# Router logits with stationary weights in four column groups, and a split first batch

## The reference

```
x = x + 0.5 * ffn(layernorm(x))          # router + 8 experts
x = x + attention(layernorm(x))          # 16 heads of 16, rms norm and rope on q and k
x = x + 0.5 * ffn(layernorm(x))          # the same router and experts again
ffn:  logits = x @ w_switch + b_switch   # (8192, 256) @ (256, 8)
      probs  = softmax(logits); routes = argmax; pos = rank of the token within its expert
      kept if pos < 512; y = relu(x @ w1[e] + b1[e]) @ w2[e] + b2[e], else y = x
attention: q, k, v = x @ wq.T, ...; q, k = rope(rms(q)), rope(rms(k))
      softmax(q k^T / 4 + 1) v, heads joined, @ wproj.T
```

## Time and profile before

| | us |
|---|---|
| median of 3 runs | 2403.99 (2400.88 to 2405.43) |
| the profiled execution | 2410.09 |
| its span, first to last instruction | 2408.2 |
| PE busy | 2194.1 (91%) |
| DVE busy | 1735.6 (72%) |
| ACT busy | 1731.4 (72%) |
| POOL busy | 977.8 (41%) |

### The profile page before, as it was taken

One profiled execution on the slowest core, in us unless ns is written; L12 is line 12 of the kernel. 1 busy time (PEld: TensorE's weight loads), 2 busy tenths in 40 slices (PEclk: granted clock), 3 DMA queues, 4 the chain that ended last, 5 costly groups with the idle time before them and its releaser, 6 DMA issues.

```text
span 2408.2 us, 36923 instructions
## 1 busy us (share of the span) xinstructions
PE 2194.1 (91%) x13224; PEld 1160.7 (48%) x13224; DVE 1735.6 (72%) x2555; ACT 1731.4 (72%) x3390; POOL 977.8 (41%) x1157
## 2 busy tenths in 40 slices
PE   6759974699899999999999999999999999996997
PEld 6738963343344434434444343444444334344896
DVE  5637755578788888798888779878887988413674
ACT  5846654358788788788878878887887887844663
POOL 3764423163273256239226623922751101113442
PEclk9999996599899999999999999999999999998998
DMA  5734331513344334334433434443343334101431
GB/s 201 261 100 172 137 105 49 91 28 82 80 81 109 57 82 101 73 58 108 98 59 86 90 76 60 98 96 59 76 106 58 68 59 107 49 17 63 158 106 62
DMA packets 144904, 218.33 MB, mean 91 GB/s; under 512 B 32225, under 2 KB 100955, under 8 KB 144465
## 3 DMA queue, kind: packets, MB, share of 16 engines
q1 hardware_dynamic: 135504, 199.01, 34.6%
q0 software_dynamic: 9216, 16.95, 2.0%
HBM read 129.59 MB, written 84.80 MB: 89 GB/s over the span
## 4 chain that ended last, share of the span: by engine, by line
PE 74%; DVE 10%; POOL 5%; issue 4%; ACT 4%; DMA 2%; SPq 1%; POOLq 0%; DVEq 0%; ACTq 0%
PE PS L800 18%; PE PS L784 17%; PE PS L767 10%; DVE NMX L1352 5%; PE PS L712 5%; PE PS L584 4%; PE PS L744 3%; PE PS L683 2%; PE PS L681 2%; PE PS L682 2%; POOL buf L1477 2%; PE PS L665 2%; PE PS L667 2%; PE PS L666 2%; PE PS L616 2%
## 5 line engine op out<-in xcount | busy, mean ns | idle before, releaser
L1352 DVE TENSOR_REDUCE NMX<-PS 128x1 f32<-128x1024 f32 x1024 | 1224.2, 1219 | 293.1 <-PE PS L767 287.7
L1043 ACT ACTIVATE PB<-PS 128x512 f32<-128x512 f32 x2048 | 1105.2, 605 | 229.6 <-PE PS L784 222.0
L784 PE MATMUL PS<-QF,KF 51*128 51x512 f32 x2048 | 802.9, 462 | 15.4 <-DMA QF<-MT 7.7
L767 PE MATMUL PS<-KF,QF 49*128 49x512 f32 x2048 | 727.5, 450 | 40.8 <-DVE NMX L1352 25.0
L784 PEld LDWEIGHTS PS<-QF,KF 51*128 51x128 f32 x2048 | 330.2, 185 | 558.2 <-ACT PB L1043 280.5
L800 PE MATMUL PS<-PB,V 128*17 128x512 f32 x4096 | 543.0, 602 | 0.2
L767 PEld LDWEIGHTS PS<-KF,QF 49*128 49x128 f32 x2048 | 317.6, 189 | 173.3 <-DVE NMX L1352 107.3
L1458 POOL TENSOR_TENSOR RS<-VE,NEGH 128x8 f32<-128x8 f32 x24 | 40.2, 1676 | 373.9 <-DVE VE L1148 373.9
L1279 DVE TENSOR_TENSOR HLR<-HL,HHR 128x512 fp32r<-128x512 f32 x128 | 88.6, 693 | 88.2 <-ACT HHR L973 88.2
L1569 POOL TENSOR_TENSOR R1R<-R,HI 128x512 fp32r<-128x512 f32 x56 | 71.7, 1282 | 183.1 <-ACT R L1010 183.1
L681 PE MATMUL PS<-W2H,HLR 128*128 128x256 f32 x512 | 143.1, 279 | 0.0
(11 more groups left out here) (173 smaller groups left out, 3331.2 us busy)
## 6 DMA issues: line engine op xcount, KB each, us to landing
W<-in_w SPq DMA_DIRECT2D x32, 1024.0 KB, 8.0
QF<-qs SPq DMA_DIRECT2D x192, 128.0 KB
KF<-qs SPq DMA_DIRECT2D x192, 128.0 KB
qs<-HI SPq DMA_DIRECT2D x64, 256.0 KB, 2.1
qs<-R1R SPq DMA_DIRECT2D x64, 256.0 KB, 2.5
buf<-ZT SPq DMA_DIRECT2D x16, 520.0 KB, 9.8
BUF<-buf SPq DMA_DIRECT2D x16, 520.0 KB, 8.5
PX<-x2d SPq DMA_DIRECT2D x8, 1024.0 KB, 5.4
```

The lines of the kernel that those rows point to most:

```text
L767: m = e.matmul(PS[:, 2 * i + half, :], QF[k][at:at + ROWS_S, p * SEQ + ti * 128:p * SEQ + ti * 128 + 128], KF[k][at:at + ROWS_S, p * SEQ + ...
L784: e.matmul(PS[:, bank, :], KF[k][at:at + ROWS_ST, p * SEQ + sbk * 128:p * SEQ + sbk * 128 + 128], QF[k][at:at + ROWS_ST, p * SEQ + th * 51 ...
L1043: e.activation(PB[j % 3][:, h * 512:(h + 1) * 512], PS[:, place["e", tile], :], ACT.Exp).then_inc(e_out, 1)
L1352: e.tensor_reduce(NMX[:, u % 2, at:at + 1], PS[:, 2 * i:2 * i + 2, :], AX.XY, ALU.max, negate=True).then_inc(s_max, 1)
```

## The change

Five things, in the diff below, cut to its core.

1. Logits: the router's weights, padded with zeros to 32 columns, are the stationary operand, once per group of 256 tokens in one of the four column groups of PE, and the transposed tokens move (256 columns). All four groups stand together at one step (`logits`); ACT copies the 128x256 result to LT, PE transposes it back in two blocks at the step `back`, and DVE's addition of the bias reads PSUM. What follows is one step later in `LATER`. The second routing's transposed tokens go to XTP instead of XTQ; the first's alternate between XTP and XTP2.
2. Batch 0's pieces: those that units 0 and 1 need (rows j = 0 and 2 of both halves) are at steps 40 to 43 of the preparation, the other four at steps 0, 1, 2, 4 of the main loop, with LO on POOL. Unit 0's load follows the first four pieces. Both halves are scaled after the second root.
3. Batch 1's preparation begins at step 4, batch 2's at step 55; `load_px` of batch 1 waits for six pieces. Values are 1 to 2 steps earlier, for batch 2 five.
4. QK has three buffers for two; `rope_out` and `sp_lo` have one semaphore per half.
5. `AGAIN_AT`: 42 matmuls after steps 13 to 21 become 26 after steps 17 to 20.

```diff
-SPLIT_AT = ((29, 31, 37, 39), (41, 43, 45, 47))
-VALUES_AT = (53, 55, 57, 59)
-FIRST_SPLIT = 4
+VALUES_AT = (52, 54, 56, 57)
+PIECES = ((29, 0, 0), (31, 0, 1), (37, 0, 2), (39, 0, 3), (41, 1, 0), (43, 1, 1), (45, 1, 2), (47, 1, 3))
+PIECES_0 = ((40, 0, 0), (41, 0, 2), (42, 1, 0), (43, 1, 2), (0, 1, 1), (1, 1, 3), (2, 0, 1), (4, 0, 3))
+BEGIN = {1: 4, 2: 55, **{b: BATCH * (b - 1) - EARLY for b in range(3, 8)}}
 FIRST = Way(...
-            logits=[9 + g for g in range(4)], shift=14, ...
+            logits=11, back=13, shift=14, ...
 LATER = Way(...
-            logits=[LEAVE + t for t in (5, 7, 9, 10)], shift=LEAVE + 11, ...
+            logits=LEAVE + 10, back=LEAVE + 11, shift=LEAVE + 12, ...
-AGAIN_AT = {**{n: 7 for n in range(13, 16)}, 16: 2, 17: 6, 18: 2, 19: 6, 20: 1, 21: 4}
+AGAIN_AT = {17: 7, 18: 7, 19: 7, 20: 5}
+def values_at(b, g):
+    return VALUES_AT[g] - (4 if b == 2 else 0) if b else BATCH - 5 + g
...
             def load_px(b):
                 if b:
-                    e.wait_ge(sp_full, 8 * b)
+                    e.wait_ge(sp_full, 8 * b if b > 1 else 6)
...
             def load_unit(u):
                 for i in range(2):
-                    e.wait_ge(st_q[i], 128 * (b + 1))
+                    e.wait_ge(st_q[i], 64 if u < 2 else 128 * (b + 1))
...
             def before(b):
-                for hf in range(2):
-                    for j in range(4):
-                        yield split_at(b, hf, j) + 3
-                        store_q(b, hf, j)
-                if b:
-                    yield EARLY + 52 if b > 1 else 56
+                yield from stores(b) if b else stores(b, 0, 4)
+                if b == 0:
+                    load_unit(0)
+                else:
+                    yield BATCH * (b - 1) + (52 if b > 1 else 57) - BEGIN[b]
                     load_unit(4 * b)
...
             def route(c):                                   # PE
-                for g in range(4):
-                    yield way.logits[g]
-                    e.wait_ge(xtq_out, 4 * c + g + 1)
-                    for i in range(2):
-                        for ch in range(2):
-                            m = e.matmul(PS[:, bank, i * 8:i * 8 + 8], xtq(c, g)[:, ch, i * 128:(i + 1) * 128],
-                                         WSW[:, ch, :], start=(ch == 0), stop=(ch == 1))
+                yield way.logits
+                e.wait_ge(xtq_out, 4 * c + 4)
+                for ch in range(2):
+                    for g in range(4):
+                        m = e.matmul(PS[32 * g:32 * g + 32, bank, 0:256], WSW[:, ch, :], xtq(c, g)[:, ch, :],
+                                     start=(ch == 0), stop=(ch == 1))
+                m.then_inc(lg_full, 1)
+                yield way.back
+                e.wait_ge(lg_out, c + 1)
+                transposes(bank, [LT[:, j * 128:(j + 1) * 128] for j in range(2)]).then_inc(lt_full, 1)
...
             def route(c):                                   # ACT
-                    e.copy(SM[k][:, 1, g * 16:g * 16 + 16], PS[:, lg_bank(c, g), 0:16]).then_inc(lg_out, 1)
+                e.copy(LT[:, :], PS[:, lg_bank(c), 0:256]).then_inc(lg_out, 1)
...
-                if n >= 2:
-                    e.wait_ge(rope_free, n - 1)
-                e.copy(QK[:, t % 2, :], PS[:, bank, :]).then_inc(qk_out, 1)
+                if n >= 3:
+                    e.wait_ge(rope_free, n - 2)
+                e.copy(QK[:, n % 3, :], PS[:, bank, :]).then_inc(qk_out, 1)
...
             def pre_x(b):                                   # DVE, batch 0
-                    if kk == 3 and b == 0:
-                        yield ROOT_AT[hf] + 1
+                if b == 0:
+                    yield ROOT_AT[1] + 1
+                    for hf in range(2):
                         e.wait_ge(rq_root, hf + 1)
                         for i in range(4):
-                            scale(e, n - 3 + i)
+                            scale(e, 4 * hf + i)
...
             for n in range(NS + LAST):                      # every engine
                 if n == 0:
-                    prepare(side, 0, 1, pre_x, values, split)
-                if r == BATCH - EARLY and b + 2 < NB:
-                    prepare(side, n, b + 2, pre_x, values, split)
+                    side.begin(n, split(0, 4, 4))
+                    prepare(side, BEGIN[1], 1, pre_x, split, values)
+                for k in range(2, NB):
+                    if n == BEGIN[k]:
+                        prepare(side, n, k, pre_x, split, values)
```

More of the change, by code:

```diff
@@ L116, in run, with pieces, prepare @@
         self.live = [s for s in self.live if s[1] is not None]
-def split_at(b, hf, j):
-    return SPLIT_AT[hf][j] + (FIRST_SPLIT if b == 1 else 0)
-def prepare(side, n, b, pre_x, *parts):
+def values_at(b, g):
+    return VALUES_AT[g] - (4 if b == 2 else 0) if b else BATCH - 5 + g
+def pieces(b, first=0, count=8):
+    table = PIECES if b else PIECES_0
+    for k in range(first, first + count):
+        at, hf, j = table[k]
+        yield k, at, hf, j, sum(p[1] == hf for p in table[:k])
+def prepare(side, n, b, pre_x, split, values=None):
     side.begin(n, pre_x(b))
-    for part in parts:
+    side.begin(n, split(b) if b else split(b, 0, 4))
+    if values is not None:
         for g in range(4):
-            side.begin(n, part(b, g))
+            side.begin(n, values(b, g))
 def build_program(nc, NB, x_in, wqkv, wproj, gq, wsw, bsw, w1, b1, w2, b2, cst, out):
@@ L714, in projected, with split @@
                 return m
-            def split(b, j):
-                for hf in range(2):
-                    yield split_at(b, hf, j)
-                    n = 8 * b + 4 * hf + j
-                    e.wait_ge(rope_out, 8 * b + 4 * hf + 4)
-                    bank = ring("split", n)
+            def split(b, first=0, count=8):
+                for k, at, hf, j, m in pieces(b, first, count):
+                    yield at
+                    e.wait_ge(rope_out[hf], 4 * b + 4)
+                    bank = ring("split", 8 * b + k)
                     take(bank)
                     transposes(bank, [QR[:, 4 * hf + i, j * 128:(j + 1) * 128] for i in range(4)]).then_inc(sp_full, 1)
-                    busy[bank] = (sp_raw, n + 1)
+                    busy[bank] = (sp_raw, 8 * b + k + 1)
             def values(b, g):
-                yield VALUES_AT[g]
+                yield values_at(b, g)
                 e.wait_ge(xt_lo, 4 * b + g + 1)
@@ L999, in pre_x, with split @@
                     e.activation(SQ[:, :], PS[:, bank, :], ACT.Square).then_inc(qk_sq, 1)
-            def split(b, j):
-                for hf in range(2):
-                    n = 8 * b + 4 * hf + j
-                    yield split_at(b, hf, j)
+            def split(b, first=0, count=8):
+                for k, at, hf, j, m in pieces(b, first, count):
+                    n = 8 * b + k
+                    yield at
                     e.wait_ge(sp_full, n + 1)
@@ L1397, in vector_program @@
                 if n == 0:
-                    prepare(side, 0, 1, pre_x, split)
-                if r == BATCH - EARLY and b + 2 < NB:
-                    prepare(side, n, b + 2, pre_x, split)
+                    side.begin(n, split(0, 4, 4))
+                    prepare(side, BEGIN[1], 1, pre_x, split)
+                for k in range(2, NB):
+                    if n == BEGIN[k]:
+                        prepare(side, n, k, pre_x, split)
                 if r == 0 and b >= 1:
```

156 lines of the change are left out of this document (83 added, 73 removed).

## The result

The changed kernel took 2365.81 us (median of 4 runs, 2361.95 to 2367.98) beside 2404.71 for the kernel before (2400.88 to 2409.74) on the same chip: ratio 0.9835, 95% interval [0.9812, 0.9858]. The forecast was 2359.4, with a range of 2343 to 2378. The profiled span went from 2408.2 to 2366.2 us.

What follows compares the result with a forecast made beforehand. Bounds were taken by stretch: TensorE full in later batches (203 of 207 us), waits exposed in batch 0's preparation. Terms -6.6 - 14 - 9 - 14 - 1 = -44.6 took 2404.0 to 2359.4 us, range 2343 to 2378.

Steps and rivals of the forecast that it cites:

- First routing: Before the first scatter: new logits blocks let ScalarE go on sooner, so the first scatter comes earlier, -6.6 us.
- Preparation: Batch 0's exposed preparation: eight tiles without a pause, four pieces left instead of six, unit 0's load earlier, -14 us.
- eight in a row: Batch 0's preparation: VectorE turns eight tiles without a stop, one per 2.59 us, from 375.4 to 396.1.
- standing alone: Unit 0's load in batch 0's preparation: 13.6 us, given no gain for running without other loads beside it.
- Rival B: Steps 0 to 8 of batch 0 give the preparation's gain back while TensorE's clock is low: 2370 us, chance 0.12.
- Batch 0: Batch 0's attention: stall near 600 us gone (-11), added transposes (+2), fewer matmuls (-1.7), later projections (+1.5): together -9 us.
- move with BEGIN, nothing changes: Batch 0's attention: batch 1's statistics shift with its preparation's start, priced at nothing.
- rival D: Stall near 600 us stays: maxima's load still late behind the store before it, only -3 of -11, 2367 us, chance 0.08.
- Later batches: Seven later batches: new logits spare TensorE 2.7 us each, partly hidden by VectorE's statistics; 2.0 taken per batch, -14 us.
- The tiling rule: Logits blocks: a change of tiling mode drains TensorE; already within the 0.98, or 0.8 us lost over seven batches.
- Tail: Last batch's exposed logits, after attention: last copy 1.5 earlier, without groups between, -1 us.
- Rival C: Batch 0 from step 17: fewer matmuls fail to raise the clock; thirty slow steps give 2437 us, chance 0.04.

Runs made afterwards that it cites:

- Run 1: Changed kernel with the old logits in both routings, the rest of the change kept: ratio 0.9889, batches 1 to 5 207.1 to 207.4 us.
- run 8: Changed kernel with POOL's first root of batch 0 waiting for the eighth sum instead of the fourth: 84.8 us from PX to the first maximum.
- run 3: Changed kernel with all eight pieces of batch 0 in the preparation and unit 0 loaded after them: ratio 0.9853.
- run 2: Changed kernel with batch 2's preparation begun at step 52 instead of 55: 2418.53 us beside 2407.96 for the changed kernel on the same chip.
- run 5: The changed kernel again, unaltered, against the kernel before: ratio 0.9754, batch 0 195.3 us.
- runs 10 and 11: Changed kernel with VectorE's statistics of batches 1 to 7 reading 8 of 256 columns, with new, then old logits: batches 205.4 to 205.5, then 206.3 to 206.6 us.
- run 12: Changed kernel without the 26 extra matmuls, first piece's LO before the second scaling, later routing from the count on one step earlier: 2356.36 us, ratio 0.9794.
- run 6: Changed kernel without the 26 bf16 matmuls at steps 17 to 20 of batch 0: ratio 0.9751, batch 0 194.4 us.

## Why the forecast came out right, and where not

The time lies in the range, and the sum came nearer than its terms did: against the forecast, the preparation gave 4 us less, batch 0 3 us more, and the later batches 3.6 less in their clean part. That the first two nearly cancel was luck.

**First routing.** Forecast -6.6, measured -5.2; in the other profiles with the new logits the first scatter stood at 40.9 to 42.2, about -5.8. The last copy of the transposed tokens of batch 0 ended at 20.71 where the forecast had 20.1 (it still waits for ScalarE's own normalization and the fourth transposes), and each block took 1.97 for 1.84, so ScalarE went on at 23.2 and not 22.4; the two transposes back took 0.70 for 0.50. Run 1 puts the whole of the gain on the logits.

**Preparation.** Forecast -14, measured -10.1 (75.2 to 79.6 us in nine profiles, so -10 to -14, against one profile of before). The step that failed is "eight in a row", one turn per 2.59 us, and a root of 7.6 behind it: beside POOL's root the fourth to sixth took 2.87, 3.23 and 3.09, and the second root took 8.6 (run 8 takes the overlap away and gets 2.59 for all). In all nine profiles the second scaling ended 31.4 to 31.6 us after the first sum, where the forecast had 29.0 (375.4 to 404.4). The first scaling's 3.19 cost nothing, since it lies in the wait for the second root. The rows of before had the sign of it: in the earlier trace rows the fourth tile's operation at 385.50 took 0.77, where the same operation elsewhere took 0.69. In the profile of the result the first sum also stood 21.9 us behind PX's issue for 20.7, so that the second scaling ended at 402.05 after a PX at 348.67, 53.4 us later and not 49.7. The last piece's LO then came out behind it by 6.6 as forecast (408.63), and the last store needed 4.08 us to land.

What spreads the nine profiles is not the turns: it is the start of the first sum (20.6 to 22.0), the time from the last store's issue to unit 0's load (2.5 to 4.3), and the load itself (12.1 to 13.9). Where -14 was reached or nearly so (75.2, 75.3 and 76.2 us), a store of 2.5 us and an early start or a short load made up for the slow turns. That standing alone gains the load nothing is borne out as far as can be told (13.6 before and 13.4 in run 3, beside other loads). Rival B did not occur: steps 0 to 7 cost 1.2 more than without the pieces (run 3).

**Batch 0.** Forecast -9, measured -12.1. By groups of 8 steps, 23.2, 25.3, 25.3, 26.0, 22.2, 22.8, 36.6, 25.2 became 23.0, 22.6, 25.9, 26.0, 25.3, 22.8, 23.0, 25.8. The stall lies in the 36.6: forecast 11, run 2 measured 11.3. The pieces cost 1.2 (run 3) where 2 was taken. Fewer bf16 matmuls, later, gave 2.1 in steps 8 to 23 (1.2 in run 5) where 1.7 was taken. The later projections cost 3.1 in steps 32 to 39 and gave back the 1.7 by which steps 48 to 63 of before (61.8) exceed those of run 2 (60.0): 1.4 net, where 1.5 was taken. What the forecast put at nothing is step 0, 3.85 before and 2.54 now: the statistics "move with BEGIN, nothing changes", but before they stood in VectorE's queue ahead of a maximum and waited for PX, as its timeline of before shows:
```profile
446.02 0.75 DVE L1138 BATCH_NORM_STATS2 ST<-PX 128x6 f32<-128x256 f32 x2 [0.83 <-DMA PX<-x2d]
```
That is 1.3. TensorE never waits for the maxima's load in the profile of the result: rival D is out.

**Later batches.** Forecast 2.0 per batch, measured 1.5 in the clean ones. The estimate that TensorE is spared 2.7 was right, and the ledger by steps finds it whole; the reason given for a part of it being hidden (VectorE's statistics) fell in runs 10 and 11. What failed is that the routing behind the logits moved one step later at no price (the forecast speaks only of the add, "one step later on VectorE, no dearer"): it costs 1.35 to 1.4 a batch in steps 0 to 7, and putting the part from the count on back gains 1.0 net (run 12). The two short spots of low clock in the profile of before (4.3 us) made up for it in the sum of spans; the medians, 38.9 apart, are not of that one execution.

**The tiling rule** that the prediction cites (the Trainium skill, "TensorEngine Tiling (Array Packing)", section Tiling Modes), put against the sum once more, would have cost 0.8 us in seven batches. The block measured 1.00 for a forecast of 0.98, so no drain is to be seen beyond 0.02; by that rule, the trace agrees only if the drain is already within the 0.98. No run isolates it.

**Tail.** Forecast -1. From the start of the last batch's normalization to its first scatter it is 16.65 us before (2169.74 to 2186.39) and in both runs with the old logits, and 15.1 to 15.2 in all eleven other profiles: -1.4, as forecast and a little more. It does not show in the whole, because from that scatter to the end it took 1.3 more here, within what this varies between profiles (221.2 to 223.1).

**Rival C** is refuted more strongly than argued: run 6 has none of these matmuls, the clock rises 8 us later, and batch 0 is as long. The steps at the low level there are hardly dearer because 17 to 19 are shorter without the matmuls (2.53 each) and only 20 and 22 longer; that they cancel to 194.4 is chance, as run 12's 193.0 without the dip shows.

**Not tested**: the third QK buffer and the values' new steps by themselves, and the two halves' scaling with the split kept.

## What to carry to other kernels

Moving a whole tail of work by one step has a price in every step where it lands: list for each its engine's load and who waits for it, also in the next batch. When a gain on the bounding engine seems half hidden, cut both profiles into groups of steps before naming a culprit; the gain was complete where it was made, and half of it lost 12 to 17 steps on. And one row of an operation that is longer than its like is a measurement of contention: use it for the overlapped case instead of the common value.

## What the hardware showed that was not expected

VectorE and GpSimd slow each other: 0.69 to 0.82 us for an operation with two operands in memory, 2.50 to 3.17 for four others, 7.3 to 8.8 for a root. Unit 0's load of twelve DMAs took 13.4 and 13.6 us with other loads beside it and 12.1 to 13.9 without. And the granted clock rose in the prologue without any matmul put there for it, only about 8 us later (487.7 for 479.3).
